# A four-stage kernel on one core: GpSimd folds 16 of the 64 search units and makes the step tables, one-hot tables are written in halves, and the order of the work is new

## The reference

```python
x = x + xattn0(layernorm(x), ctx, Wq, bq, Wk, bk)   # attention weights from ctx alone, applied to x
x = x + ffn0(layernorm(x), w_fc, w_proj)             # both weights quantised first
x = x + xattn1(layernorm(x), fside, ctx)             # int8 smooth-quant gate/up/down, silu
x = x + ffn1(layernorm(x), Wq, keys, e_down, e_up)   # product keys: top 8 of 128 by 128
# the quantiser of ffn0, for each block of 64 weights (8192 blocks):
for s in linspace(0.4, 1.0, 16):
    scale = base * s
    deq = clip(round(wb / scale), -15, 15) * scale
    err = sum((deq - wb) ** 2)        # over the 64 weights
    keep the scale of the smallest err
# then: h = relu(x @ wq_fc.T); out = (h * h) @ wq_proj.T
```

## Time and profile before

| | before |
|---|---|
| median of 3 runs | 389.44 us (389.33 to 390.71) |
| the profiled execution | 389.69 us, its span 387.9 us |
| TensorE, VectorE, ScalarE, GpSimd busy | 342.5, 343.1, 247.7, 99.6 us |
| TensorE's granted clock, mean | 0.98 of full speed |

### The profile page before, as it was taken

One profiled execution on the slowest core, in us unless ns is written; L12 is line 12 of the kernel. 1 busy time (PEld: TensorE's weight loads), 2 busy tenths in 40 slices (PEclk: granted clock), 3 DMA queues, 4 the chain that ended last, 5 costly groups with the idle time before them and its releaser, 6 DMA issues.

```text
span 387.9 us, 8250 instructions
## 1 busy us (share of the span) xinstructions
PE 342.5 (88%) x3222; PEld 250.7 (65%) x3222; DVE 343.1 (88%) x868; ACT 247.7 (64%) x371; POOL 99.6 (26%) x148
## 2 busy tenths in 40 slices
PE   2997898598968969999979889998999999989997
PEld 2454554144423425778978767887888887778876
DVE  4999999999999999368788999999999999999940
ACT  3899999979999982227457797755766654011000
POOL 3010011340660343121001104256424158601000
PEclk9999999869999999999989999999999999999999
DMA  8930000000000007100000000000000000000000
GB/s 254 358 132 2 1 0 2 1 1 0 2 1 0 2 0 235 37 0 3 0 2 0 3 0 3 1 3 2 0 18 14 2 15 4 2 15 2 18 15 27
DMA packets 11142, 11.40 MB, mean 29 GB/s; under 512 B 608, under 2 KB 10592, under 8 KB 11104
## 3 DMA queue, kind: packets, MB, share of 16 engines
q1 hardware_dynamic: 11104, 10.88, 8.8%
HBM read 9.83 MB, written 1.05 MB: 28 GB/s over the span
## 4 chain that ended last, share of the span: by engine, by line
DVE 53%; PE 25%; ACT 10%; issue 8%; DMA 2%; SPq 1%; POOL 0%; DVEq 0%; ACTq 0%
DVE arena L1627 10%; PE pair L898 7%; PE pair L736 5%; DVE i L1966 4%; DVE arena L1617 3%; DVE s L1960 3%; DVE arena L2026 3%; PE pair L590 3%; DVE arena L2022 2%; ACT arena L1167 2%; ACT arena L1164 2%; DVE XN L1552 2%; PE pair L884 2%; DMA arena<-in_L_ffn_keys_dram 2%; DVE pk L1981 2%
## 5 line engine op out<-in xcount | busy, mean ns | idle before, releaser
L1627 DVE TENSOR_REDUCE arena<-arena 128x16 f32<-128x1024 f32 x64 | 75.8, 1207 | 0.0
L862 PE MATMUL pair<-arena,EDT 128*128 128x256 f32 x256 | 60.2, 383 | 0.0
L898 PE MATMUL pair<-EU,arena 128*128 128x256 f32 x256 | 58.4, 382 | 0.6 <-DVE arena L2050 0.6
L898 PEld LDWEIGHTS pair<-EU,arena 128*128 128x128 f32 x256 | 47.9, 190 | 7.4 <-issue 1.0
L862 PEld LDWEIGHTS pair<-arena,EDT 128*128 128x128 f32 x256 | 47.1, 190 | 6.5 <-ACT arena L1418 0.2
L608 PE MATMUL pair<-arena,WQ 128*128 128x512 fp8e4 x112 | 35.8, 403 | 13.8 <-ACT arena L1164 8.8
L620 PE MATMUL pair<-arena 128*128 128x512 fp8e4 x128 | 40.5, 399 | 2.9 <-DVE arena L1617 2.9
L452 POOL TENSOR_TENSOR arena<-arena 128x512 f32<-128x512 f32 x20 | 27.4, 1383 | 45.0 <-ACT arena L1410 45.0
L1150 ACT ACTIVATE arena<-arena,clip_bias 128x1024 fp8e4<-128x1024 f32 x32 | 37.7, 1187 | 0.3 <-PE pair L620 0.3
L1164 ACT ACTIVATE arena<-pair,sq_bias 128x1024 f32<-128x1024 f32 x32 | 36.6, 1145 | 1.3 <-PE pair L620 1.3
L1418 ACT ACTIVATE arena<-pair 128x512 f32<-128x512 f32 x32 | 19.0, 598 | 26.4 <-PE pair L862 26.4
(11 more groups left out here) (200 smaller groups left out, 642.6 us busy)
## 6 DMA issues: line engine op xcount, KB each, us to landing
arena<-in_L_ffn_e_down_dram SPq DMA_DIRECT2D x1, 2048.0 KB, 12.2
EU<-in_L_ffn_e_up_dram SPq DMA_DIRECT2D x1, 2048.0 KB, 9.3
arena<-in_L_ffn_w_fc_dram SPq DMA_DIRECT2D x2, 512.0 KB, 5.3
X<-in_x_dram SPq DMA_DIRECT2D x1, 1024.0 KB, 5.9
arena<-in_L_ffn_w_proj_dram SPq DMA_DIRECT2D x1, 1024.0 KB, 13.7
GUW<-in_fside_BxS2xS_dram SPq DMA_DIRECT2D x1, 1024.0 KB, 12.4
out_dram<-arena SPq DMA_DIRECT2D x8, 128.0 KB, 1.7
CTX<-in_ctx_dram SPq DMA_DIRECT2D x1, 512.0 KB, 4.8
```

The source lines that it names most:

```text
L862: last = pe.matmul(bk2(4 + i % 2)[:, r, :], EDT[:, k, at:at + P], xT4[:, b % 2, k, :], start=(k == 0), stop=(k == 1))
L898: last = pe.matmul(bk2(7)[:, n, :], PR[:, n, e, :], EU[:, e, :], start=(e == 0), stop=(e == EROWS - 1))
L1627: dve.tensor_reduce(err[:, g // NS % 2, :, g % NS], squares, AX.X, ALU.add).then_inc(s["reduced"], 1)
```

## The change

- `halved(g)` is now true for g = 1, 5, 9, ..., 61: GpSimd folds these 16 units from 1024 to 512 columns, and VectorE's `sum_error` reads the folded half.
- `step_tables(k)` moves from VectorE's list to GpSimd's: groups 0 to 3 at its start, the others between folds.
- `one_hots(t)` becomes `one_hots(t, half)`: for each half of `oh` one instruction of 2048 elements and three of 512 for `wc`, eight instructions where there were two. A half waits only for the scatter of the same half of the tile before, and `scatter` for its own half.
- GpSimd waits until all four chunks are quantised before `square_hidden(8)`.
- ScalarE's wait for the `e_down` transposes in `square(g)` stands only in units with g % 5 = 3 behind unit 24.
- All five lists have a new order. Most of it is shown below. In short: `prepare(1)` stands ahead of `split(0)`; `relu(6)` and `relu(7)` stand behind `square(63)`; `ffn2(0, 0)` and `ffn2(1, 0)` stand ahead of `w_transposed(3)`, and `ffn2(0, 1)`, `ffn2(1, 1)` right behind it, with `ffn1(9)` to `ffn1(15)` after them; the `c_` chains of batches 0 and 1 run side by side, and `ffn2(2, ...)`, `ffn2(3, ...)` stand behind both `c_a_transposed`.

```diff
-            return g < 0
+            return g % 4 == 1
...
+            def step_tables(k):
+
+                for j in (2 * k, 2 * k + 1):
+                    sign = -1.0 if on_act(j) else 1.0
+                    ins = pool.tensor_scalar(stepI[:, j, :], ident[:, :], sign * STEPS[j] / GRID, None, ALU.mult)
+                    if k:
+                        sign = 1.0 if on_act(j - 2) else -1.0
+                        ins = pool.tensor_scalar(stepN[:, j - 2, :], ident[:, :], sign * STEPS[j - 2] / GRID, None,
+                                                ALU.mult)
+                ins.then_inc(s["steps"], 1)
+
+            step_tables(0)
+            step_tables(1)
+            step_tables(2)
+            step_tables(3)
             scale_weights(1)
+            fold(1)
+            step_tables(4)
+            fold(5)
+            step_tables(5)
+            step_tables(6)
+            fold(9)
+            step_tables(7)
+            fold(13)
             split(1)
+            fold(17)
+            fold(21)
             scale_quantised(0)
             scale_weights(2)
+            dequantise(0)
+            fold(25)
             split(2)
-            dequantise(0)
+            fold(29)
+            fold(33)
+            scale_quantised(1)
+            fold(37)
+            dequantise(1)
+            scale_weights(3)
+            fold(41)
             square_hidden(0)
+            split(3)
+            fold(45)
             square_hidden(1)
-            scale_quantised(1)
+            fold(49)
+            scale_quantised(2)
             square_hidden(2)
-            scale_weights(3)
-            dequantise(1)
-            split(3)
             square_hidden(3)
+            fold(53)
+            dequantise(2)
+            fold(57)
             square_hidden(4)
+            fold(61)
             square_hidden(5)
             square_hidden(6)
-            scale_quantised(2)
-            dequantise(2)
             square_hidden(7)
 
+            pool.wait_ge(s["wquant"], NCH)
             square_hidden(8)
             square_hidden(9)
             square_hidden(10)
@@ -454,29 +490,25 @@
...
             def scatter(b, n, half):
 
                 t = 2 * b + n
-                if half == 0:
-                    pe.wait_ge(s["d_onehot"], t + 1)
+                pe.wait_ge(s["d_onehot"], 2 * t + half + 1)
...
             pe.wait_ge(s["wT_e"], 6)
             ffn1(8)
+            pe.wait_ge(s["squared"], NU)
+            pe.wait_ge(s["hsq"], 8)
+            ffn2(0, 0)
+            ffn2(1, 0)
+            w_transposed(NCH - 1)
+            gate_weights_transposed(0)
+            gate_weights_transposed(1)
+            pe.wait_ge(s["wT_e"], 8)
+            ffn2(0, 1).then_inc(s["f2_t"], 1)
+            ffn2(1, 1).then_inc(s["f2_t"], 1)
+            c_x_transposed(0)
             ffn1(9)
             ffn1(10)
-            pe.wait_ge(s["squared"], NU)
-            gate_weights_transposed(0)
-            pe.wait_ge(s["hsq"], 8)
-            ffn2(0, 0)
-            w_transposed(NCH - 1)
+            c_x_transposed(1)
+            gate_weights_transposed(2)
+            gate_weights_transposed(3)
+            c_factors(0)
             ffn1(11)
-            pe.wait_ge(s["wT_e"], 8)
-            ffn2(0, 1).then_inc(s["f2_t"], 1)
+            c_factors(1)
             ffn1(12)
             ffn1(13)
-            c_x_transposed(0)
-            ffn2(1, 0)
-            c_factors(0)
+            c_row_scales(0)
             ffn1(14)
-            ffn2(1, 1).then_inc(s["f2_t"], 1)
+            c_quantised_transposed(0)
             ffn1(15)
-            c_row_scales(0)
-            gate_weights_transposed(1)
-            c_quantised_transposed(0)
-            gate_weights_transposed(2)
-            gate_weights_transposed(3)
+            c_row_scales(1)
             c_first(0)
-            c_x_transposed(1)
+            c_quantised_transposed(1)
+            c_first(1)
+            c_a_transposed(0)
+            c_a_transposed(1)
             pe.wait_ge(s["hsq"], 16)
             ffn2(2, 0)
-            c_a_transposed(0)
+            c_factors2(0)
             ffn2(2, 1, (0,))
-            c_factors(1)
+            c_factors2(1)
+            ffn2(3, 0)
+            c_row_scales2(0)
             ffn2(2, 1, (1,)).then_inc(s["f2_t"], 1)
-            c_factors2(0)
-            ffn2(3, 0)
-            ffn2(3, 1, (0,))
-            c_row_scales(1)
-            c_row_scales2(0)
             c_quantised2_transposed(0)
-            c_quantised_transposed(1)
+            c_row_scales2(1)
             c_second(0)
-            c_first(1)
-            ffn2(3, 1, (1,)).then_inc(s["f2_t"], 1)
+            c_quantised2_transposed(1)
+            ffn2(3, 1).then_inc(s["f2_t"], 1)
             pre(0)
...
-                if g > QF_LATE:
+                if g > QF_LATE and g % QDEPTH == 3:
...
+            relu(5)
             square(63)
             weights_out(2)
+            relu(6)
+            relu(7)
...
             prepare(0)
             scale_weights(0)
             clip_round(0)
+            prepare(1)
+            split(0)
             clip_round(2)
-            split(0)
+            first_stats()
...
-            def one_hots(t):
-
+            def one_hots(t, half):
+
+                o, k = slice(NO // 2 * half, NO // 2 * half + NO // 2), slice(16 * half, 16 * half + 16)
                 if t:
-                    dve.wait_ge(s["d_c_t"], 4 * t)
-                dve.tensor_tensor(oh, iotaI.unsqueeze(1).to_broadcast([P, NO, P, NG]), over(t, 1, P), ALU.is_equal)
+                    dve.wait_ge(s["d_c_t"], 4 * t - 2 + 2 * half)
+                column = packT[:, t % 2, 1, k].rearrange("p (o g) -> p o g", g=NG).unsqueeze(2).to_broadcast(
+                    [P, NO // 2, P, NG])
+                dve.tensor_tensor(oh[:, o], iotaI.unsqueeze(1).to_broadcast([P, NO // 2, P, NG]), column, ALU.is_equal)
                 dve.wait_ge(s["d_mask"], t + 1)
-                parts = packT[:, t % 2, 2:5, :].rearrange("p c (o g) -> p c o g", g=NG).unsqueeze(3).to_broadcast(
-                    [P, 3, NO, JW, NG])
-                dve.tensor_tensor(wc, msk.unsqueeze(1).to_broadcast([P, 3, NO, JW, NG]), parts, ALU.mult
-                                  ).then_inc(s["d_onehot"], 1)
+                for c in range(3):
+                    part = packT[:, t % 2, 2 + c, k].rearrange("p (o g) -> p o g", g=NG).unsqueeze(2).to_broadcast(
+                        [P, NO // 2, JW, NG])
+                    ins = dve.tensor_tensor(wc[:, c, o], msk[:, o], part, ALU.mult)
+                ins.then_inc(s["d_onehot"], 1)
 
             def weigh(t, quarters):
...
```

More of the change, by code:

```diff
@@ L690, in _ @@
             unit(35)
+            x1_transposed(2)
             unit(36)
+            unit(37)
             x1_transposed(3)
-            unit(37)
-            ffn1(0)
             unit(38)
-            ffn1(1)
-            ffn1(2)
             unit(39)
             unit(40)
-            ffn1(3)
             unit(41)
+            ffn1(0)
             unit(42)
             unit(43)
+            ffn1(1)
             unit(44)
@@ L708, in _ @@
             unit(47)
+            ffn1(2)
             unit(48)
@@ L711, in _ @@
             unit(50)
-            ffn1(4)
+            ffn1(3)
             unit(51)
@@ L715, in _ @@
             unit(53)
+            ffn1(4)
             unit(54)
+            unit(55)
             ffn1(5)
-            unit(55)
             unit(56)
+            unit(57)
             ffn1(6)
-            unit(57)
-            ffn1(7)
             unit(58)
@@ L727, in _ @@
             unit(62)
+            w_transposed(2)
             unit(63)
-            w_transposed(2)
+            ffn1(7)
             def ffn2(b, o, tiles=range(TPB)):
@@ L1282, in _ @@
             square(44)
-            relu(3)
             square(45)
@@ L1286, in _ @@
             square(46)
+            relu(1)
             square(47)
@@ L1293, in _ @@
             square(50)
+            relu(2)
             square(51)
+            clip_round(55)
             square(52)
+            relu(3)
+            square(53)
+            clip_round(57)
+            square(54)
             relu(4)
-            clip_round(55)
-            square(53)
-            square(54)
-            clip_round(57)
-            relu(5)
             square(55)
@@ L1304, in _ @@
             square(56)
-            relu(6)
             square(57)
@@ L1462, in _ @@
+            std(0, 2, "ln4")
+            tokens_out(0)
+            c_root(2)
             std(3, 2, "ln3")
+            queries(0, (0,))
+            c_diag(2)
+            queries(0, (1,))
             std(1, 2, "ln4")
-            gate(0, 3, 5)
+            gate(0, 0, 2)
             c_integers(2)
             tokens_out(1)
-            gate(0, 5, 6)
+            gate(0, 2, 4)
             c_row_scales_out(2)
-            gate(0, 6, 7)
             c_integers_out(2)
-            gate(0, 7, 8)
+            gate(0, 4, 8)
@@ L1472, in _ @@
             c_silu(2)
```

(14 more changed lines are left out.)

631 lines of the change are left out of this document (299 added, 332 removed).

## The result

The changed kernel takes 395.13 us (median of 4 runs, 394.11 to 395.66), beside 390.07 us for the kernel before in the same session: ratio 1.0124, 95% interval 1.0088 to 1.0160. It is slower by 5 us, where 386.0 was predicted. The profiled execution is one of 395.66 us with a span of 393.9, 1.8 around it as before. It is the slowest of the four, 0.5 above their median, near enough for its trace to stand for them.

What follows compares the result with a forecast made beforehand. No one engine bounds it all: ScalarE and VectorE fill the search, TensorE is fullest behind it. -2.4 of lead at pre(0) and -1.0 of gaps make -3.4 us: 386.3 for the profiled run, 386.0 median; range 382 to 390.3.

Steps and rivals of the forecast that it cites:

- the sum's first term: At pre(0), start of product-key work: TensorE's lead over the kernel before, counted as -2.4 us.
- the sum's -3.4 us: Whole kernel: predicted saving, -2.4 us of lead at pre(0) and -1.0 of TensorE gaps.
- the 1.7 and the 1.0: Behind pre(0): 1.7 us of batch 1's TensorE steps already done, and 1 us less TensorE gaps from 200 to 240.
- 27.3: Middle, x2(0) to ffn2(2, 0): time for both batches' chains, taken between 23.3 and 34.8 us.
- The gain of 2.0 us: End of the search: last square at 142.3 us, 2.0 earlier (0.9 lost to 4.6 gained).
- the predicted 143.9: Behind the search: TensorE's start of ffn1(8), 2.6 us earlier than before (0.5 to 5.2).
- The surplus of 11 us: Search: VectorE's net relief from folds and step tables, some 11 us (from -4.2 to 12.3).
- where I took 1.5: Search: VectorE's loss to GpSimd blocking its roundings, 1.5 us, up to 16.5 if every fold delayed it wholly.
- the 0.75 that the prediction set as a sign: Search: VectorE's roundings should stay below 0.75 us in the mean beside GpSimd's folds.
- Taken at 4 us of VectorE's time: Product-key stage: extra VectorE cost of one-hot tables in halves over eight tiles, 4 us (3.2 to 7.2).
- the pair of chains that stalls TensorE: Rival, middle: both batches' work adds up to 34.8 us, TensorE idles 7.5 more than counted: 393.5 us; chance 0.11.

Runs made afterwards that it cites:

- e1: Changed search (folds, step tables on GpSimd, new order), with all stages behind it as in the kernel before: 388.46 us, ratio 0.9967.
- e11: Second run of the changed search with all stages behind it as in the kernel before: 387.41 us, ratio 0.9925.
- e6: Changed kernel with TensorE work moved ahead of its waits for c_quantised_transposed(3) and pre(3): 401.02 us, ratio 1.0282.
- e13: Changed kernel with batch 3's steps between rounding and x3 put ahead of product-key work on VectorE: 394.66 us, ratio 1.0114.
- e8: Kernel before with only the step tables moved from VectorE to the head of GpSimd's list, no folds: 390.30 us, ratio 1.0011.
- e9: Changed search without folds, step tables still on GpSimd, stages behind it as in the kernel before: 391.78 us, ratio 1.0062.
- e3: Kernel before with only the one-hot tables made in halves, all eight tiles: 391.92 us, ratio 1.0055.
- e7: Changed kernel with ffn1(15), ffn2(2, 0) and half of ffn2(2, 1) filling TensorE's gaps in the side-by-side chains: 395.51 us, ratio 1.0160.

## Why the prediction was wrong, by its steps

**The step that failed is the sum's first term**: "at `pre(0)` TensorE leads by 0.7 + 1.7 = 2.4 us, VectorE by 6". Between the profiled executions the sum's -3.4 us came out as +6.0, 9.4 us off: 2.6 of them had arisen by `pre(0)`, which came 1.9 us later than before and not 0.7 earlier, and 6.8 behind it, where the 1.7 and the 1.0 were to be saved. From `pre(0)` to the last result TensorE takes 185.3 us, 181.2 before; 178.5 was predicted.

**Up to `pre(0)`.** It was predicted at 203.4 and came at 206.02. Up to `x2(0)` it went better than said (157.64, not 158.8). The chain side by side took 29.5 us from `x2(0)` to `ffn2(2, 0)`, not 27.3, and from there to `pre(0)` 18.9, not 17.3; 1.0 of these 1.6 is `ffn2(2, 0)` itself, 4.73 us for the 3.74 of the earlier trace rows. That is -1.2 + 2.2 + 1.6 = 2.6. And the mark to beat was not 204.13: on the changed search the old middle starts `pre(0)` at 200.23 (e1) and 201.01 (e11). Against that, putting the chains side by side costs 5 to 5.8 us at the step that opens the product-key work.

**Batch 1's earliness was banked as if it were time.** It bought some: 4.9 us up to `pre(2)`, more than the 1.7 + 1.0 that I counted. Then 8.5 are lost up to `pre(3)`, a stretch that the prediction put at nothing without a reason. The two reorderings tried there bought nothing that the time shows: in e6 a wait that was taken away came back dearer, in e13 at another step. Where in the stretch the 8.5 us lie is told under experiment 13. What they consist of is known in part: VectorE's longer work ahead of `x3(3)` (4.4), and on TensorE a low clock behind the wait at 278.64, where the steps up to 285.42 took 6.8 us and the same four 3.7 in e1. No run takes these apart.

**Search.** The gain of 2.0 us was right in size (388.46 and 387.41, beside 389.87 and 389.52), and TensorE was there at 142.48 for `ffn1(8)`, ahead of the predicted 143.9. The reason was half right: with the old order VectorE has nothing to give (e8), in the new one it needs the folds (e9, 4 us). The surplus of 11 us that I gave VectorE is not there. The roundings took 0.80 us in the mean instead of 0.697, 3.2 us over 32, where I took 1.5, beside folds of 1.29 us in the mean, not 1.03; 0.80 is also above the 0.75 that the prediction set as a sign. The rest, read from the traces before and after: the sixteen layer-norm products in the search (`XN`, 128x256) took 9.0 us and not 5.8, nearly all of it in two pairs that ran beside GpSimd (1.74 and 2.88 us for 0.73); VectorE is idle for 8.9 of the first 15 us, not 5.6, as in the new order it waits there for the loads for 6.3 us (4.3 before) and for ScalarE for 2.4 (1.1); and it is up to date at the end, where the last choosing is over at 149.0 and not 154.7, 5.7 us earlier beside 3.5 for the last square. The Trainium skill, "SBUF — State Buffer", section "Who interferes with whom", says that a `tensor_reduce` never contends with GpSimd and a `tensor_scalar` in a two-port mode does; the trace agrees: whole sums took 1.208 us in the mean with 16 folds beside them (1.21 in the earlier trace rows), the rounding at 66.51 took 1.58.

**Halves.** Taken at 4 us of VectorE's time. From start to start a half takes 1.13 + 1.01 us where nothing holds it, 4.3 a tile against 3.9, and 1.1 more where GpSimd weighs beside it (4 halves of 16): 8 x 0.4 + 4 x 1.1 = 7.6 us, or 6.5 more than before, where one of the eight `wc` was held up too (2.83 us for 1.75). It was the held-up ones that I left out. In the kernel's time it is 2.0 us in the old order (e3) and 0.5 in the new one (395.13 against 394.58, not told from none).

**The baseline.** The sum was made from one execution of before. Its last square is the latest of four with the old search, by up to 2.7 us, and part of the granted clock in that search was 0.87. Its `pre(0)` is not out of line (204.13, beside 202.71 in e3 and 204.79 in e8), so the baseline explains an error of a us or two at most, and not the sign.

**The rivals.** The one that ends slower, the pair of chains that stalls TensorE, had the place, the sign and nearly the size (393.5); its mechanism, work that adds up to 34.8 us, was not what happened (28.6 from `x2(0)` to `c_a_transposed(0)` and `(1)`), and filling the gaps (e7) gave nothing. That its number came so near is luck. It had 0.11. The range left out the outcome by 5 us.

What stays open: whether a key order exists that uses an early batch 1 and keeps batch 3's chain at 36.8 us, and how the 4 to 5 us of the middle divide between the chains side by side and the `ffn2` that stand ahead of `pre(0)`. The fastest version run is the changed search with everything behind it as before: 388.46 and 387.41 us, ratios 0.9967 and 0.9925.

## What to carry to other kernels

Time the step that opens the next stage, not the mean progress of all batches: two chains side by side finish together, but the first one finishes later, and the large products that waited for both then stand ahead of the next stage. A lead on a full engine counts only as far as the list behind it was checked for waits down to the end, and two reorderings must be measured as a square, since one may be good only with the other.

## What the hardware showed

TensorE's clock fell after its own gaps. Windows of the changed kernel around the waits ahead of `ffn2(2, 0)` and around the one of 2.60 us (the clock stands behind the five busy times, 1.00 being 2.4 GHz):

```profile
180.00:185.00 5.00, 3.40 (x24) 1.92 (x22) 1.60 (x5) 3.99 (x6) 2.08 (x2) 1.00 0.03 7
185.00:188.00 3.00, 1.80 (x9) 1.76 (x10) 2.27 (x10) 2.26 (x4) 0.00 (x0) 0.63 0.00 0
188.00:192.00 4.00, 4.00 (x32) 4.00 (x32) 1.41 (x9) 1.68 (x6) 0.00 (x0) 0.85 0.00 0
...
275.00:280.00 5.00, 2.40 (x93) 2.21 (x86) 4.90 (x30) 4.37 (x8) 0.37 (x2) 0.79 0.04 15
280.00:285.00 5.00, 5.00 (x24) 3.65 (x24) 4.97 (x15) 2.58 (x3) 4.70 (x7) 0.53 0.04 15
```

From 180 to 185 TensorE was busy for 3.4 of 5 us and at 2.4 GHz; then, after three gaps (1.41, 1.10 and 1.57 us), it ran at a mean between its two levels, and `ffn2(2, 0)` paid 1 us. At 280 to 285, behind a gap of 2.60 us, it was near 1.2 GHz, and eight matmuls of `up` took 3.73 us, 1.95 at 307.44. A gap thus costs more than itself.

GpSimd holds up the smallest of VectorE's instructions as well: the 128x2 product of L1865 at 164.05 took 1.04 us (0.16 the three other times), exactly as long as the GpSimd product that started at 164.04, and three `wc` instructions 2.23 us for 1.08. The Trainium skill, same section, says that a VectorE instruction with two inputs in SBUF contends with a GpSimd instruction that reads it. The trace agrees.
